# Two chained convolution layers on one core: the square-root table load and one normalisation move to other places

## The chip, the cores and the metric

The kernel runs on one core of a Trainium2 chip. The metric is the time of one execution in microseconds (us); less is better. Engines go by the names that the profile gives them: PE (TensorE, matrix products), DVE (VectorE), ACT (ScalarE), POOL (GpSimd), SP (the engine that issues most transfers).

## The reference

The input x has 16 images of 32 channels, 48 by 48 pixels. Two layers follow one another, each a normalisation over 16 groups of 2 channels (`_gn`), a convolution and an addition to its input:

```python
x = x + _L0_conv_ref(_gn(x), L0_conv_weight, L0_conv_bias)   # 9x9, kernels are Gaussians made from 3 numbers each
x = x + _L1_conv_ref(_gn(x), L1_conv_weight)                 # 5x5, reflected at the edges
...
m = jnp.mean(g, axis=(2, 3, 4), keepdims=True)
s = jnp.var(g, axis=(2, 3, 4), keepdims=True)
return ((g - m) / jnp.sqrt(s + eps)).reshape(v.shape)
```

The Gaussian kernels are computed in the kernel: sine and cosine, an exponential over 9x9 taps, a sum per kernel and a division by it.

## The kernel before, in words

The images are worked in four quads of four (`qd` 0 to 3). Partitions hold 4 row phases of 32 channels. Each layer uses a Winograd form along the rows: layer 1 turns the normalised rows `P` into 8 streams (`s32_1`, shown as `s`), multiplies each with its own weights and combines 8 products into 6 rows. Streams and weights are split into a high and a low half in 16 bits (`hi`, `lo`; `wh`, `wl`, which are both in `whl`), and PE adds the products hi x wh, lo x wh and hi x wl. In the trace a cast `hi<-s` on ACT makes a high half (`high_half`), a subtraction `lo<-s,hi` on DVE the low one (`low_half`). For weights it is `whl<-work` or `whl<-arg` on ACT (`high_kernel`, line 1182) and the same names on DVE at line 568 (`low_kernel`).

Every engine has its instructions in an order written out by hand, and the engines wait for one another with semaphores. Nothing reorders them when the kernel runs.

The change lies in the first quad, where nothing of the weights is ready yet. There the streams are made in the order 1, 2, 0, 7, 3, 4, 5, 6, each as soon as it can be. PE takes for each stream first the five taps that were made ("made": 15 products, three times five), later the four that mirror others ("turned": 12 products). The order on PE starts with stream 1 made, two products that turn its weights around (line 1533), stream 2 made, the same turning for stream 2, stream 1 turned, stream 0 made, and so on. Stream 6 made is the seventh of the made ones, and its high half is the last that ACT makes in this quad (`high_half(1, 0, 7)`).

Streams 1 and 2 of the first quad aren't formed from `P`. PE sums rows of x in the banks (`near_rows`), and ACT (`first_stream1`, line 1118) and DVE (`first_stream2`, line 699) only scale them. All other streams need `P`, which ACT writes in `normalise1` (line 1131), two instructions for each of the four images of the quad. `norm_done[1]` counts the images, and DVE waits for four before `first_half`.

The scale `gsc` and the offset `gof` of the first quad come from the variance. DVE takes the reciprocal square root by a first guess from the bits of the number and further steps (`first_guess`, `first_newton`, `second_root`, `first_scales`), and these small steps stand between the larger sums over the weights (`outer_blocks`, `all_blocks`, `tap_pairs`). For every later quad, `small_stats` on DVE waits for a square root that ACT makes (`standard_deviation`, line 1104), and takes a reciprocal and one Newton step. The table that ACT needs for the square root is loaded once, at line 1278, just ahead of `high_half(1, 0, 7)`. `small_stats(1, 1)` stands on DVE ahead of `low_half(1, 0, 7)`.

POOL normalises the last image of the second quad (line 1393).

Of the kernel before, what the change touches and what calls it, by code (L numbers as in the profile page):

```python
# [26 lines left out]
ALU = mybir.AluOpType  # L27
# [14 lines left out]
IMG = 2  # L42
# [48 lines left out]
NF = len(OUT_FACTORS)  # L91
EPS = 1e-5
ROUND = 12582912.0
ROOT_BITS = float(0x5F3759DF + 6 * 2**23)
ROOT3 = 0.375 ** 0.5
TWO_PI = 6.2831850
SMALL = 9

# [53 lines left out]
def build(nc, x, w0, bias, w1, tables, out):  # L152
    with ExitStack() as ctx:
# [182 lines left out]
        def block1(b):  # L336
            return ker[:, :, b * P:(b + 1) * P]
# [100 lines left out]
        def _(dve):  # L438
# [159 lines left out]
            def step(ins):  # L598

                step_count[0] += 1  # L600
                ins.then_inc(first_step_done, 1)

            def step_landed():
                dve.wait_ge(first_step_done, step_count[0])
# [10 lines left out]
            def first_variance():  # L615
                dve.wait_ge(stat_mm, 1)
                step_landed()
                step(tt(var[1][:, :], STAT[1][:, QI:], msq[1][:, :], ALU.add))
                step_landed()
                step(ts(vare[1][:, :], var[1][:, :], 0.0, EPS, ALU.max, ALU.add))  # L620

            def first_guess():
                step_landed()
                step(ts(rcp[1][:, :].bitcast(I32), vare[1][:, :].bitcast(I32), -0.5, ROOT_BITS, ALU.mult, ALU.add))
                step_landed()
                step(stt(msq[1][:, :], vare[1][:, :], -0.5 / (X_SCALE * X_SCALE), rcp[1][:, :], ALU.mult, ALU.mult))

            def first_newton():
                step_landed()
                step(tt(var[1][:, :], msq[1][:, :], rcp[1][:, :], ALU.mult))  # L630
                step_landed()
                step(stt(rcp[1][:, :], var[1][:, :], 1.5, rcp[1][:, :], ALU.add, ALU.mult))

            def second_root():

                step_landed()
                step(stt(msq[1][:, :], vare[1][:, :], ROOT3 / (X_SCALE * X_SCALE), rcp[1][:, :], ALU.mult, ALU.mult))
                step_landed()
                step(tt(var[1][:, :], msq[1][:, :], rcp[1][:, :], ALU.mult))

            def first_scales():
                step_landed()
                step(stt(msq[1][:, :], var[1][:, :], -1.25 / ROOT3, var[1][:, :], ALU.add, ALU.mult))
                step_landed()
                stt(gsc[1][:, :], msq[1][:, :], 1.875, rcp[1][:, :], ALU.add, ALU.mult).then_inc(small[1], SMALL - 2)
                dve.wait_ge(small[1], SMALL - 2)
                stt(off1[:, :], first_mean, -NEAR_OFFSET, gsc[1][:, :], ALU.mult, ALU.mult).then_inc(small[1], 1)
                stt(gof[1][:, :], first_mean, -1.0, gsc[1][:, :], ALU.mult, ALU.mult).then_inc(small[1], 1)

            def small_stats(c, n):  # L650
# [10 lines left out]
                tt(var[c][:, :], ex2, msq[c][:, :], ALU.add).then_inc(small[c], 1)  # L661
                dve.wait_ge(small[c], at + 3)
                ts(vare[c][:, :], var[c][:, :], 0.0, EPS, ALU.max, ALU.add).then_inc(small[c], 1)
                dve.wait_ge(std_done[c], n + 1 if c == 2 else n)
                nc.vector.reciprocal(rcp[c][:, :], std[c][:, :]).then_inc(small[c], 1)

                dve.wait_ge(small[c], at + 5)
# [24 lines left out]
            def first_stream2():  # L692

                dve.wait_ge(near_mm, 2)
                dve.wait_ge(s_done[1], 1)
                for h in range(2):
                    at = slice(h * TILES1, (h + 1) * TILES1)
                    by_image = gsc[1][:, h * IMG:(h + 1) * IMG].unsqueeze(1).unsqueeze(3).to_broadcast([P, TILES1, IMG, W])
                    ins = tt(by_image1(s32_1[:, 2, :])[:, at, :, :], by_image1(banks[:, NEAR_BANK[2], 0:OUTN])[:, at, :, :], by_image, ALU.mult)
                ins.then_inc(s_done[1], 1)  # L700

            def first_half(key, which, one, other):

# [158 lines left out]
            def first_quad():  # L862
# [7 lines left out]
                outer_blocks(0)  # L870
                first_variance()
                all_blocks(0)
                first_guess()
                outer_blocks(1)
                first_newton()
                all_blocks(1)
                second_root()
                tap_pairs()
                first_scales()
                kernel_sum()  # L880
# [5 lines left out]
                kernel_scale()  # L886
                low_half(1, 0, 0)
                scaled(block1(1), "block1")
                first_stream2()
                low_kernel(1)  # L890
                made_two()
                low_half(1, 0, 1)
                low_kernel(2)
                scaled(block1(0), ("weights", 0))
# [181 lines left out]
        def _(act):  # L1076
# [156 lines left out]
            near_factors((0,))  # L1233
            channel_sums(1, 0, range(2, 4))
            kernel_exponentials()
            near_factors((1, 2))
            opposite_rows()
            first_stream1()
            high_half(1, 0, 0)
            normalise1(0, range(2))  # L1240
            high_kernel(1)
            normalise1(0, range(2, 3))
            high_half(1, 0, 1)
            high_kernel_two()
            turned_kernel(1, 0)
            normalise1(0, range(3, 4))
            turned_kernel(1, 1)
            high_kernel(0)
            turned_kernel(2, 0)
# [24 lines left out]
            turn_kernel(5, wh)  # L1274
            high_kernel(6)
            turn_kernel(5, wl)

            nc.scalar.activation(warm[:, :], bias_c[2][:, :], ACT.Sqrt)
            high_half(1, 0, 7)
            standard_deviation(1, 1)  # L1280
            turn_kernel(6, wh)
# [339 lines left out]
```

## Time and profile before

| | |
|---|---|
| time, median of 3 | 244.48 us (244.37 to 244.97) |
| the profiled execution | 244.16 us |
| its span, from the first to the last instruction | 242.4 us |
| PE busy | 232.7 us, 96% of the span |
| DVE busy | 211.3 us, 87% |
| ACT busy | 154.0 us, 64% |
| mean granted clock of TensorE | 1.000 |

The times are those of whole executions; the trace is of one more execution and shows 1.76 us less between its first and last instruction than its own time. Starts in the trace are counted from the first instruction. Two instructions behind one another on DVE or ACT overlap a little in the trace (the second starts about 0.08 us before the end of the first), so that what one costs its engine is the distance of the starts.

### The profile page before, as it was taken

The page shows a single profiled execution, that of the slowest core. Times are in us where ns is not written, and L with a number is a line of the kernel's source. Part 1 is how long each engine was busy: PE and PEld are TensorE (multiplying, and loading weights), DVE is VectorE, ACT ScalarE, POOL GpSimd, SP SyncE. Part 2 cuts the span into 40 slices and gives each one's busy share as a digit, 9 for nine tenths or more (in the row PEclk, how much of TensorE's full clock was granted, in tenths as well). Part 3 has the DMA queues.
Part 4 walks back from the last instruction along what each step waited for, and adds up shares of the span by engine and source line. Part 5 has one row for each costly group of instructions (what it writes and reads, how often), then busy time and mean ns, then how long its engine had stood idle before and what let it go on. Part 6 is the DMA issues. An engine that isn't in the chain of part 4 may idle for free.

```text
span 242.4 us, 4154 instructions
## 1 busy us (share of the span) xinstructions
PE 232.7 (96%) x1441; PEld 144.9 (60%) x1441; DVE 211.3 (87%) x463; ACT 154.0 (64%) x330; POOL 4.4 (2%) x12
## 2 busy tenths in 40 slices
PE   5997999899999999999999999999999999999995
PEld 5854666555565665555666665556666665655554
DVE  4997999699999999999989998999997459978943
ACT  6858898999399567999537592537359003569210
POOL 1000000050000000000000000000000000000000
DMA  6980031320025000003412000062020001521123
GB/s 212 378 329 1 14 75 45 77 55 0 0 53 159 6 1 0 0 3 101 147 64 97 0 4 0 17 187 108 1 100 0 0 0 48 162 101 55 48 97 97
DMA packets 8709, 17.24 MB, mean 71 GB/s; under 512 B 3312, under 2 KB 5616, under 8 KB 8688
## 3 DMA queue, kind: packets, MB, share of 16 engines
q1 hardware_dynamic: 7712, 16.64, 20.9%
q10 hardware_dynamic: 976, 0.34, 0.6%
q8 instruction: 11, 0.18, 0.3%
q14 instruction: 10, 0.08, 0.1%
HBM read 5.57 MB, written 4.72 MB: 42 GB/s over the span
## 4 chain that ended last, share of the span: by engine, by line
PE 68%; DVE 21%; ACT 6%; issue 4%; DMA 1%; DVEq 0%; ACTq 0%
PE banks L1478 34%; PE banks L1495 33%; DVE X L796 4%; DVE lo L763 2%; DVE whl L568 2%; ACT P L1131 1%; DVE work L563 1%; DMA prm<-in_w 1%; DVE arg L507 1%; DVE s L733 1%; DVE partU L749 1%; ACT whl L1182 1%; DVE s L499 1%; ACT hi L1154 1%; ACT junk L1098 1%
## 5 line engine op out<-in xcount | busy, mean ns | idle before, releaser
L1478 PE MATMUL banks<-hi,whl 128*128 128x360 f16 (+4 forms) x576 | 99.1, 320 | 3.2 <-ACT whl L1182 1.9
L1478 PEld LDWEIGHTS banks<-hi,whl 128*128 128x128 f16 x576 | 55.9, 99 | 38.2 <-ACT whl L1182 2.5
L1478 PE MATMUL banks<-lo,whl 128*128 128x376 f16 (+4 forms) x288 | 51.6, 320 | 0.5 <-DVE lo L763 0.5
L1098 ACT ACTIVATE junk<-X 128x576 bf16<-128x576 f32 x56 | 38.1, 681 | 2.2 <-DVE X L796 0.5
L1478 PEld LDWEIGHTS banks<-lo,whl 128*128 128x128 f16 x288 | 28.0, 98 | 17.8 <-DVE lo L763 1.1
L1495 PE MATMUL banks<-lo,wh 128*128 128x384 f16 (+1 forms) x165 | 31.8, 323 | 0.0
L1495 PE MATMUL banks<-hi,wh 128*128 128x384 f16 (+1 forms) x165 | 31.8, 323 | 0.0
L1495 PE MATMUL banks<-hi,wl 128*128 128x384 f16 (+1 forms) x165 | 31.8, 323 | 0.0
L1154 ACT CAST hi<-work 128x416 f16<-128x416 f32 x32 | 16.6, 538 | 19.9 <-PE banks L1495 14.1
L1154 ACT CAST hi<-s 128x384 f16<-128x384 f32 x32 | 15.3, 508 | 17.8 <-DVE s L730 12.1
L1144 ACT ACTIVATE work<-work,gof,gsc 128x26 f32<-128x26 f32 (+1 forms) x48 | 23.3, 577 | 3.6 <-DVE gof L674 3.6
L1495 PEld LDWEIGHTS banks<-hi,wl 128*128 128x128 f16 x165 | 15.9, 97 | 10.5
L1495 PEld LDWEIGHTS banks<-lo,wh 128*128 128x128 f16 x165 | 15.9, 97 | 10.5
L1495 PEld LDWEIGHTS banks<-hi,wh 128*128 128x128 f16 x165 | 16.0, 98 | 10.4
L763 DVE TENSOR_TENSOR lo<-work,hi 128x416 f16<-128x416 f32 x32 | 17.4, 584 | 1.6 <-ACT hi L1154 1.5
L796 DVE SCALAR_TENSOR_TENSOR X<-pd,X 128x384 f32<-128x384 f32 x36 | 18.1, 558 | 0.0
L796 DVE SCALAR_TENSOR_TENSOR X<-ps,X 128x384 f32<-128x384 f32 x36 | 18.1, 558 | 0.0
L1131 ACT ACTIVATE P<-X,gof,gsc 128x336 f32<-128x336 f32 x30 | 17.7, 658 | 0.5 <-DVE gof L674 0.5
L763 DVE TENSOR_TENSOR lo<-s,hi 128x384 f16<-128x384 f32 x32 | 16.4, 552 | 0.4
L786 DVE SCALAR_TENSOR_TENSOR ps<-banks,mb 128x384 f32<-128x384 f32 x12 | 6.6, 554 | 8.3 <-PE banks L1478 7.6
L1165 ACT ACTIVATE mb<-banks,bias 128x384 f32<-128x384 f32 x12 | 6.9, 572 | 8.2 <-PE banks L1478 8.2
L1098 ACT ACTIVATION_READ_ACCUMULATOR junk<-X 128x1 f32 x56 | 10.5, 187 | 0.0
(141 smaller groups left out, 231.1 us busy)
## 6 DMA issues: line engine op xcount, KB each, us to landing
X<-in_x SPq DMA_DIRECT2D x8, 576.0 KB, 9.5
out<-X SPq DMA_DIRECT2D x7, 576.0 KB, 3.0
work<-X SPq DMA_DIRECT2D x8, 432.0 KB, 3.8
whl<-work SPq DMA_DIRECT2D x24, 64.0 KB, 2.0
work<-X SPq DMA_DIRECT2D x8, 144.0 KB, 3.6
stage<-in_w SPq DMA_DIRECT2D x1, 640.0 KB, 7.2
work<-X SPq DMA_DIRECT2D x32, 12.0 KB, 2.3
out<-X SPq DMA_DIRECT2D x1, 384.0 KB, 2.6
```

Source lines behind the costliest of these rows:

```text
L499: done(tt(ca[:, at, :].rearrange("p k (e o) -> p k e o", o=C), centre.unsqueeze(1).to_broadcast([P, n, NE, C]), ak[:, at, :].unsqueeze(2). ...
L568: tt(made_taps(wl, i), weight1(i), made_taps(wh, i), ALU.subtract).then_inc(wl1_done, 1)
L763: tt(lo[c][:, i, :], src, hi[c][:, i, :], ALU.subtract).then_inc(lo_done[c], 1)
L786: stt(ps[1][:, :], product1(qd, k), f, mb[1][:, :], ALU.mult, ALU.add).then_inc(mid_done[1], 1)
L796: stt(out1(qd, k), tiled1(src[1][:, :]), factors[g][i], out1(qd, k), ALU.mult, ALU.add).then_inc(out_done[1], 1)
L1098: nc.scalar.activation(waste, image(n, m), function, accum_out=sums[c][:, col:col + 1]).then_inc(sums_done[c], 1)
L1131: ins = nc.scalar.activation(dst, src, ACT.Identity, bias=gof[1][:, i:i + 1], scale=gsc[1][:, i:i + 1])
L1144: ins = nc.scalar.activation(dst[:, :, d0:d1_:ds_], src[:, :, s0:s1:ss], ACT.Identity, bias=gof[2][:, i:i + 1], scale=gsc[2][:, i:i + 1])
L1154: nc.scalar.copy(hi[c][:, i, :], src).then_inc(hi_done[c], 1)
L1165: nc.scalar.activation(mb[1][:, :], src, ACT.Identity, bias=bias_c[1 if g == 0 else 2][:, 0:1], scale=FIRST1[g]).then_inc(m_read[1], 1)
L1478: ins = nc.tensor.matmul(dst[:, :, o0:o1], w[1][:, i, t * P:(t + 1) * P], src[:, :, o0 + dx:o1 + dx], start=(first and part == 0 and t == ...
L1495: ins = nc.tensor.matmul(dst, wbuf[2][:, i, j * P:(j + 1) * P], src[:, rows, t:t + W], start=(part == 0 and t == 0), stop=(part == 2 and t ...
```

## The change

It has four parts.

1. The reciprocal square root of the first quad is taken as in later quads. ACT makes the square root, and DVE a reciprocal and one Newton step. The table for the square root is loaded right behind the exponentials of the weights, no longer ahead of `high_half(1, 0, 7)`.
2. ACT normalises one image ahead of `high_kernel(1)`, where it did two, and the others follow later.
3. The fourth image of the first quad (`QI - 1`) is normalised by DVE, with two `tensor_scalar` instructions between `made_two` and `low_half(1, 0, 1)`.
4. On DVE `low_kernel(1)` stands ahead of `first_stream2`.

```diff
-                step(ts(vare[1][:, :], var[1][:, :], 0.0, EPS, ALU.max, ALU.add))
-
-            def first_guess():
-                step_landed()
-                step(ts(rcp[1][:, :].bitcast(I32), vare[1][:, :].bitcast(I32), -0.5, ROOT_BITS, ALU.mult, ALU.add))
+                ts(vare[1][:, :], var[1][:, :], 0.0, EPS, ALU.max, ALU.add).then_inc(small[1], 4)
+
+            def first_root():
+                dve.wait_ge(std_done[1], 1)
+                step(nc.vector.reciprocal(rcp[1][:, :], std[1][:, :]))
                 step_landed()
                 step(stt(msq[1][:, :], vare[1][:, :], -0.5 / (X_SCALE * X_SCALE), rcp[1][:, :], ALU.mult, ALU.mult))
...
-            def second_root():
...
             def first_scales():
-                step_landed()
-                step(stt(msq[1][:, :], var[1][:, :], -1.25 / ROOT3, var[1][:, :], ALU.add, ALU.mult))
-                step_landed()
-                stt(gsc[1][:, :], msq[1][:, :], 1.875, rcp[1][:, :], ALU.add, ALU.mult).then_inc(small[1], SMALL - 2)
+                dve.wait_ge(first_step_done, MARK["first newton"])
+                stt(gsc[1][:, :], var[1][:, :], 1.5, rcp[1][:, :], ALU.add, ALU.mult).then_inc(small[1], SMALL - 6)
...
+            def normalise_last():
+
+                i = QI - 1
+                h, m = i // IMG, i % IMG
+                dve.wait_ge(x_loaded[h], 16)
+                dve.wait_ge(small[1], SMALL)
+                dve.wait_ge(pads_zero, 2)
+                for t in range(TILES1):
+                    dst = P1[:, TILES1 * h + t, :].rearrange("p (r m x) -> p r m x", m=IMG, x=W)[:, 1 - t:ROWS1 - t, m, :]
+                    src = image(h, m)[:, (M1 - 1) * t:(M1 - 1) * t + ROWS1 - 1, :]
+                    ins = ts(dst, src, gsc[1][:, i:i + 1], gof[1][:, i:i + 1], ALU.mult, ALU.add)
+                ins.then_inc(norm_done[1], 1)
...
                 outer_blocks(0)
                 first_variance()
                 all_blocks(0)
-                first_guess()
                 outer_blocks(1)
+                first_root()
+                all_blocks(1)
                 first_newton()
-                all_blocks(1)
-                second_root()
                 tap_pairs()
                 first_scales()
...
                 scaled(block1(1), "block1")
+                low_kernel(1)
                 first_stream2()
-                low_kernel(1)
                 made_two()
+                normalise_last()
                 low_half(1, 0, 1)
...
             kernel_exponentials()
+            nc.scalar.activation(warm[:, :], bias_c[2][:, :], ACT.Sqrt)
+            standard_deviation(1, 0)
             near_factors((1, 2))
...
             high_half(1, 0, 0)
-            normalise1(0, range(2))
+            normalise1(0, range(1))
             high_kernel(1)
-            normalise1(0, range(2, 3))
+            normalise1(0, range(1, 2))
             high_half(1, 0, 1)
             high_kernel_two()
+            normalise1(0, range(2, 3))
             turned_kernel(1, 0)
-            normalise1(0, range(3, 4))
             turned_kernel(1, 1)
...
             turn_kernel(5, wl)
-
-            nc.scalar.activation(warm[:, :], bias_c[2][:, :], ACT.Sqrt)
             high_half(1, 0, 7)
```

The order on ACT, from the exponentials (`arg<-arg`) to the high half of the weights of stream 2 (`whl<-work` with 384 and 256 elements), before the change:

```order
L1178 ACTIVATE arg<-arg 128x768
L1110 ACTIVATE factors<-tab 128x128 x2
L1199 CAST opposite<-tab 128x128
L1118 ACTIVATE s_1<-banks,off,gsc 128x2x48 x4
L1154 CAST hi<-s_1 128x384
L1131 ACTIVATE P<-X,gof,gsc 128x7x48 x4
L1182 CAST whl<-work 128x640
L1131 ACTIVATE P<-X,gof,gsc 128x7x48 x2
L1154 CAST hi<-s_1 128x384
L1188 CAST whl<-work 128x384
L1188 CAST whl<-work 128x256
```

and with the change:

```order
L1179 ACTIVATE arg<-arg 128x768
L1237 ACT_TABLE_LOAD
L1237 ACTIVATE warm<-bias 128x1
L1105 ACTIVATE std<-vare 128x4
L1111 ACTIVATE factors<-tab 128x128 x2
L1200 CAST opposite<-tab 128x128
L1119 ACTIVATE s_1<-banks,off,gsc 128x2x48 x4
L1155 CAST hi<-s_1 128x384
L1132 ACTIVATE P<-X,gof,gsc 128x7x48 x2
L1183 CAST whl<-work 128x640
L1132 ACTIVATE P<-X,gof,gsc 128x7x48 x2
```

A table load and a square root are new behind the exponentials, and the weights of stream 1 (`whl<-work` 128x640) stand behind two normalising instructions, not four.

On DVE, from the scaling of block 1 (`arg<-arg,rs`) to the first part that needs `P` (`partA<-P`), before:

```order
L551 TENSOR_TENSOR arg<-arg,rs 128x5x128
L699 TENSOR_TENSOR s_1<-banks,gsc 128x192 x2
L568 TENSOR_TENSOR whl<-work,whl 128x640
L559 SCALAR_TENSOR_TENSOR work<-arg,work 128x384
L559 SCALAR_TENSOR_TENSOR work<-arg,work 128x256
L763 TENSOR_TENSOR lo<-s_1,hi 128x384
L568 TENSOR_TENSOR whl<-work,whl 128x640
L551 TENSOR_TENSOR arg<-arg,rs 128x5x128
L705 TENSOR_TENSOR partA<-P 128x4x96
```

and with the change:

```order
L549 TENSOR_TENSOR arg<-arg,rs 128x5x128
L566 TENSOR_TENSOR whl<-work,whl 128x640
L687 TENSOR_TENSOR s_1<-banks,gsc 128x192 x2
L557 SCALAR_TENSOR_TENSOR work<-arg,work 128x384
L557 SCALAR_TENSOR_TENSOR work<-arg,work 128x256
L700 TENSOR_SCALAR P<-X,gsc,gof 128x7x48 x2
L764 TENSOR_TENSOR lo<-s_1,hi 128x384
L566 TENSOR_TENSOR whl<-work,whl 128x640
L549 TENSOR_TENSOR arg<-arg,rs 128x5x128
L706 TENSOR_TENSOR partA<-P 128x4x96
```

The two instructions `P<-X,gsc,gof` are new here, and stream 2 (`s_1<-banks,gsc`) stands behind the low half of the weights of stream 1.

On ACT at the end of the quad's weights, where `high_half(1, 0, 7)` is the cast `hi<-s_1` and `standard_deviation(1, 1)` is `std<-vare`, before:

```order
L1182 CAST whl<-work 128x640
L1196 COPY work<-whl 128x512
L1278 ACT_TABLE_LOAD
L1278 ACTIVATE warm<-bias 128x1
L1154 CAST hi<-s_1 128x384
L1104 ACTIVATE std<-vare 128x4
```

and with the change:

```order
L1183 CAST whl<-work 128x640
L1197 COPY work<-whl 128x512
L1155 CAST hi<-s_1 128x384
L1105 ACTIVATE std<-vare 128x4
```

Here the load and the activation behind it are gone.

## Rows read from the trace of the kernel before

**Rows 1.** The page: busy tenths of PE in 40 equal slices of the span

```profile
PE   5997999899999999999999999999999999999995
```

**Rows 2.** Waits of PE, 15 to 60 us: us in total, times, longest us

```profile
PE banks L1478 <- ACT whl L1182: 1.9, 1, 1.9
PE banks L1478 <- ACT hi L1154: 1.2, 2, 0.9
PE banks L1478 <- DVE lo L763: 0.5, 1, 0.5
```

**Rows 3.** Timeline, 44 to 49 us: start us, us, engine, line, operation [idle before]

```profile
45.65 1.28 ACT L1278 ACT_TABLE_LOAD   x1
...
46.14 0.17 DVE L663 TENSOR_SCALAR vare<-var 128x4 f32<-128x4 f32 x1
...
47.05 0.49 ACT L1154 CAST hi<-s 128x384 f16<-128x384 f32 x1
47.45 0.20 ACT L1104 ACTIVATE std<-vare 128x4 f32<-128x4 f32 x1
...
47.69 0.18 DVE L665 RECIPROCAL rcp<-std 128x4 f32<-128x4 f32 x1 [1.38 <-ACT std L1104]
47.90 0.16 DVE L668 SCALAR_TENSOR_TENSOR msq<-vare,rcp 128x4 f32<-128x4 f32 x1
```

**Rows 4.** Timeline of ACT, 9 to 19 us, and PE's start on stream 2

```profile
9.59 1.90 ACT L1178 ACTIVATE arg<-arg 128x1152 f32<-128x1152 f32 x2 [0.54 <-DVE arg L507]
...
14.89 1.40 ACT L1118 ACTIVATE s<-banks,off,gsc 128x96 f32<-128x96 f32 x4 [2.81 <-DVE gof L648]
...
16.74 2.34 ACT L1131 ACTIVATE P<-X,gof,gsc 128x336 f32<-128x336 f32 x4
...
18.98 0.71 ACT L1182 CAST whl<-work 128x640 f16<-128x640 f32 x1
...
22.54 0.95 PE L1478 MATMUL banks<-hi,whl 128*128 128x384 f16 x5
```

**Rows 5.** Timeline of DVE, 12.5 to 15 us

```profile
13.16 0.42 DVE L519 TENSOR_TENSOR work<-work,arg 128x256 f32<-128x256 f32 x1
...
13.77 0.42 DVE L524 TENSOR_TENSOR work<-work 128x256 f32<-128x256 f32 x1
14.10 0.15 DVE L643 SCALAR_TENSOR_TENSOR msq<-var 128x4 f32<-128x4 f32 x1
14.36 0.16 DVE L645 SCALAR_TENSOR_TENSOR gsc<-msq,rcp 128x4 f32<-128x4 f32 x1
...
14.64 0.15 DVE L648 SCALAR_TENSOR_TENSOR gof<-mom,gsc 128x4 f32<-128x4 f32 x1
```

**Rows 6.** Timeline of DVE, 17 to 25 us

```profile
17.45 0.82 DVE L551 TENSOR_TENSOR arg<-arg,rs 128x640 f32<-128x640 f32 x1
18.19 0.61 DVE L699 TENSOR_TENSOR s<-banks,gsc 128x192 f32<-128x192 f32 x2
19.72 0.83 DVE L568 TENSOR_TENSOR whl<-work,whl 128x640 f16<-128x640 f32 x1 [0.92 <-ACT whl L1182]
20.46 0.89 DVE L559 SCALAR_TENSOR_TENSOR work<-arg,work 128x384 f32<-128x384 f32 x2
21.27 0.55 DVE L763 TENSOR_TENSOR lo<-s,hi 128x384 f16<-128x384 f32 x1
...
24.32 0.56 DVE L705 TENSOR_TENSOR partA<-P 128x384 f32<-128x384 f32 x1 [0.79 <-ACT P L1131]
```

**Rows 7.** Groups by line and form, DVE and POOL: busy us, mean ns of one

```profile
L475 DVE TENSOR_TENSOR rnd<-sc 128x64 f32<-128x64 f32 x1 | 0.2, 220 | 0.0
L456 DVE TENSOR_SCALAR rnd<-turn 128x64 f32<-128x64 f32 x1 | 0.2, 195 | 0.0
L582 DVE TENSOR_SCALAR osc<-tab,wpow 128x4 f32<-128x4 f32 x1 | 0.2, 219 | 0.0
L1393 POOL TENSOR_SCALAR P<-X,gsc,gof 128x336 f32<-128x336 f32 x2 | 3.5, 1766 | 47.4 <-DVE gof L674 47.4
```

**Rows 8.** Stretch of an earlier table load: busy us of PE, PEld, DVE, ACT, POOL; PEclk, DMA share, GB/s

```profile
3.80:5.20 1.40, 1.40 (x8) 1.40 (x8) 1.31 (x6) 1.37 (x3) 0.00 (x0) 1.00 1.03 387
```

More of the change, by code:

```diff
@@ L93 @@
 ROUND = 12582912.0
-ROOT_BITS = float(0x5F3759DF + 6 * 2**23)
-ROOT3 = 0.375 ** 0.5
 TWO_PI = 6.2831850
@@ L630, in first_newton @@
                 step(tt(var[1][:, :], msq[1][:, :], rcp[1][:, :], ALU.mult))
-                step_landed()
-                step(stt(rcp[1][:, :], var[1][:, :], 1.5, rcp[1][:, :], ALU.add, ALU.mult))
-            def second_root():
-                step_landed()
-                step(stt(msq[1][:, :], vare[1][:, :], ROOT3 / (X_SCALE * X_SCALE), rcp[1][:, :], ALU.mult, ALU.mult))
-                step_landed()
-                step(tt(var[1][:, :], msq[1][:, :], rcp[1][:, :], ALU.mult))
+                MARK["first newton"] = step_count[0]
             def first_scales():
-                step_landed()
-                step(stt(msq[1][:, :], var[1][:, :], -1.25 / ROOT3, var[1][:, :], ALU.add, ALU.mult))
-                step_landed()
-                stt(gsc[1][:, :], msq[1][:, :], 1.875, rcp[1][:, :], ALU.add, ALU.mult).then_inc(small[1], SMALL - 2)
+                dve.wait_ge(first_step_done, MARK["first newton"])
+                stt(gsc[1][:, :], var[1][:, :], 1.5, rcp[1][:, :], ALU.add, ALU.mult).then_inc(small[1], SMALL - 6)
                 dve.wait_ge(small[1], SMALL - 2)
@@ L663, in small_stats @@
                 ts(vare[c][:, :], var[c][:, :], 0.0, EPS, ALU.max, ALU.add).then_inc(small[c], 1)
-                dve.wait_ge(std_done[c], n + 1 if c == 2 else n)
+                dve.wait_ge(std_done[c], n + 1)
                 nc.vector.reciprocal(rcp[c][:, :], std[c][:, :]).then_inc(small[c], 1)
```

## The prediction, written before the changed kernel ran

> **What bounds the kernel now.** I read the page's slices first. PE is busy in nine tenths or more of every slice from 24 us on, except at the very end [rows 1]. So time can only be won in PE's few waits, or where PE starts. The list of PE's waits names them for 15 to 60 us [rows 2]: 1.9 us for the high half of stream 1's weights, 1.2 us in two waits for a high half of a stream (0.9 the longest), 0.5 us for a low half. The timeline tells where they lie. The first is the start of the convolutions near 19.7 us: ACT casts the weights of stream 1 at 18.98 for 0.71 us [rows 4]. The 0.9 and the 0.5 lie around 47 to 49 us, on one stream: ACT loads a table at 45.65 for 1.28 us, and only then, at 47.05, makes the last high half of the first quad; and the low half of the same stream stands on DVE behind the small statistics, where DVE sat idle 1.38 us for the square root [rows 3]. Between these two places PE doesn't wait, but DVE does hardly either, so it is DVE's lead or lag that arrives at 45 us. DVE's own waits ahead of that are 0.92 us for the same weights and 0.79 us for `P` [rows 6].
>
> I follow three clocks, then: when the weights of stream 1 are cast, by how much DVE is earlier at `partA`, and by how much the low half of the last stream is earlier.
>
> **Part 1, the new root.** The exponentials end at 11.49 [rows 4]. The load starts 0.02 later; the old place took 1.40 us from the load to the next real instruction [rows 3], so the square root starts at 12.91. From there to the reciprocal it took 47.69 - 47.45 = 0.24 and to the next step 0.21 [rows 3]: reciprocal 13.15, next 13.36. The sum `work<-work,arg` follows 0.08 behind, at 13.44, where it stood at 13.16 [rows 5]. It takes 0.42, and the next sum needs its end: 13.87 instead of 13.77. The one Newton product fits beside it. Where there were two steps behind the pair sum (at 0.33 and 0.59 behind it), there is now one, at 0.33: `gsc` at 14.20 instead of 14.36, and `gof` 0.28 later at 14.48 instead of 14.64 [rows 5]. The gain is 0.15 us, for ACT, whose stream 1 starts 0.25 behind `gof` (14.74), and for DVE. The factors and the reversed identity that ACT makes behind the square root come about 1.5 us later than they did, by roughly 13.7, in ACT's idle 2.81 us [rows 4]. The root itself is thus nearly a draw: DVE waits about 0.4 us for it and saves five small steps.
>
> **Part 2, the order on ACT.** Four normalising instructions took 18.98 - 16.74 = 2.24 us, two take 1.12 [rows 4]. The cast starts at 16.74 - 0.15 + 1.12 = 17.71 instead of 18.98, and PE 1.27 us earlier. PE needs the second stream 22.54 - 18.98 = 3.56 behind the cast [rows 4], so at 21.27.
>
> **Parts 3 and 4, DVE to `partA`.** The scaling of block 1 starts at 17.30 and takes 0.74 (the distance of starts, [rows 6]); DVE then waits for the cast, which before it followed 19.72 - 18.98 = 0.74 behind, until 17.71 + 0.74 = 18.45. The low half of the weights takes 0.74 (19.19), stream 2 its 0.61 less the overlap of 0.08, which makes 0.53 (19.72), its weights 0.81 (20.53). Stream 2 now ends at about 19.8, its high half on ACT is there by about 20.3, and PE wants it at 21.27: this new wait of ACT costs nothing, and would cost something only where its cover of 0.9 us were gone.
>
> No row shows a normalisation on DVE. From above, a TENSOR_TENSOR of 64 elements takes 220 ns [rows 7] and one of 384 takes 560 [rows 6], or 506 at 336 elements. A TENSOR_SCALAR of 64 takes 195 [rows 7], less than its neighbour; one of 4 takes 170 [rows 3]. That slope, 0.4 ns an element, gives 310 ns at 336. One whose scalar is a tensor took 219 ns against those 170 [rows 3, 7], so 50 more for the pointers. The bounds are 0.36 and 0.56 us; I take 0.40, since the TENSOR_SCALAR rows lie on the lower slope. Less the overlap the pair costs 0.64 us, at the upper bound 0.95. The Trainium skill, "VectorE: DVE Perf Modes", section "The perf-mode tier table", lets a `tensor_scalar` on fp32 in SBUF run at twice the rate of a `tensor_tensor`, which agrees with the value taken.
>
> DVE goes on at 21.17; the low half takes 0.47, the weights' low half and the next scaling 0.74 each, and `partA` starts at 23.12 instead of 24.32. `P` of the third image is written on ACT by about 22.2, so the wait of 0.79 is gone. DVE is 1.20 us earlier (0.90 by the upper bound), PE 1.27; PE may wait for the difference.
>
> **The end of the quad.** Both engines carry that lead to 45 us. There the load is gone. ACT's high half starts right behind its stream, about 1.4 us earlier beyond the lead; PE doesn't wait for it. The variance starts at 46.14 and ends at 46.31 [rows 3]; the square root could follow 0.04 later and the reciprocal 0.24 after that: 46.59, where it stood at 47.69. So all that hangs on it, `gof`, the last low half and everything of DVE behind, gains 1.10 us beyond the lead. PE comes to that low half earlier by its lead of 1.2 and by the 0.9 us that it no longer waits for the high half, 2.1 in all, and finds it 2.3 earlier: of the wait of 0.5 some 0.4 is left. This wait is what is late next, and so DVE sets the sum, not PE.
>
> **The sum.** 1.20 + 1.10 = 2.30 us, with the upper bound of the normalisation 2.00. From there all engines are earlier by the same amount; the work until about 79 us hangs on DVE and PE as it did, and PE is full afterwards [rows 1]. Against the profiled execution of 244.16 that is 241.86. The median of before lies 0.32 above it, so I forecast 242.2 us.
>
> **The rivals.**
>
> *DVE at one element a cycle* (0.56 us for one normalising instruction): 2.00 us are gained, 242.5. For it: the operand is in rows of 48, and no such row was seen. Against it: the two TENSOR_SCALAR rows. Chance 0.2.
>
> *Only one half arrives.* Either the 1.10 us is eaten where PE, DVE and ACT meet again between 49 and 79 us, or DVE's lead is lost before 45 us because ACT falls behind with its own part; 1.1 or 1.2 us remain, 243.3. For it: DVE runs nearly without a gap there, so a new wait of DVE has no cover. Against it: each wait that I looked at moves with what it waits for. Chance 0.1.
>
> *A dearer load.* At 3.80 to 5.20 us ACT was busy 1.37 of 1.40 us around a load, with the DMA engines full (share 1.03) and the clock at 1.00, the 2.4 GHz level [rows 8]; so a load costs 1.28 us and nothing behind it, also while x is being loaded. If it cost twice that at the new place, the reciprocal, and with it both streams, would come 1.3 us later, and 1.0 us of gain would be left: 243.5. The Trainium skill, "ScalarE: Activation LUTs", section "What ACT_TABLE_LOAD costs", counts a drain of 1.38 us behind each load, 2.66 us in all, and advises to count every switch at that. The rows of this trace don't show the drain: the next real instruction followed 1.40 us behind the start of the load [rows 3]. Chance 0.05.
>
> *Slower.* The one row of this very operation is POOL's, 1766 ns [rows 7]. If DVE needed as much, the pair would cost 2 x 1.69 = 3.38 us, 2.74 more than I count, all of it on the path to `partA`: DVE would be 1.54 us later at `partA` and 0.44 later at the end, 244.9. It decides from 1.55 us for one instruction on. POOL's other durations don't speak for DVE. Chance 0.03.
>
> *No change:* the leads are made, but a transfer or the last low half holds PE where it was. The turned weights go by DMA behind ACT's copies, which move with the rest. Chance 0.04.
>
> **How the numbers follow.** My forecast, with the two-fold rate on DVE, has 0.52: 242.2, and 0.2 us to either side for the estimates in it. More gain than 2.9 us has 0.06: it would need a wait that I count as kept to go, since PE's own lead and its two waits at 47 to 49 us add up to 1.2 + 0.9 + 0.5 = 2.6. The range takes in the one-element case (242.5), the half gains (243.3) and a little below the forecast: 241.6 to 243.4. About 0.3% (0.7 us) is what a measurement of this kernel can tell from no change. Faster by more has 0.92, within it 0.04, slower 0.04.
>
> **What would show it.** The square root near 12.9 and `gof` near 14.5 us; the cast of stream 1's weights near 17.7 and PE's first convolution product near 18.5; `P<-X` on DVE at about 0.4 us each; `partA` near 23.1 with no wait ahead of it; at about 45 to 47 us a single wait of PE, of about 0.4 us, for the low half of the last stream, and DVE's reciprocal near 45.4 with a wait of some 0.3. The prediction is wrong if `partA` is earlier but the reciprocal at the end of the quad isn't, if PE shows a new wait between 20 and 44 us of more than 0.2, or if the lead at 60 us is gone at 100.

## The result, and the profile after

The changed kernel takes 242.06 us (median of 4, 241.99 to 242.10) where the kernel before takes 244.46 us beside it: a ratio of 0.9897, with a 95% interval of 0.9880 to 0.9914. A second measurement on another chip gave 242.59 us (median of 5, 242.02 to 242.85) against 244.43, a ratio of 0.9916 (0.9898 to 0.9935). The forecast was 242.2 us, in a range of 241.6 to 243.4. The profiled execution of the changed kernel took 242.1 us with a span of 240.3.

PE's waits between 15 and 60 us, the view of [rows 2], now read (us in total, times, longest us):

```profile
PE banks L1479 <- ACT whl L1183: 0.6, 1, 0.6
PE banks L1479 <- DVE lo L764: 0.5, 1, 0.5
PE banks L1479 <- ACT hi L1155: 0.3, 1, 0.3
```

The wait for the weights of stream 1 shrank by 1.3 us. Of the two waits for a high half the longer one (0.9) is gone. The wait for the low half is as long as it was.

The timeline of ACT shows the new place of the table load and the order behind it (start us, us, engine, line, operation):

```profile
11.64 1.28 ACT L1237 ACT_TABLE_LOAD   x1
12.93 0.20 ACT L1237 ACTIVATE warm<-bias 128x1 f32<-128x1 f32 x1
13.04 0.19 ACT L1105 ACTIVATE std<-vare 128x4 f32<-128x4 f32 x1
...
14.87 1.40 ACT L1119 ACTIVATE s<-banks,off,gsc 128x96 f32<-128x96 f32 x4 [1.06 <-DVE gof L636]
...
16.72 1.22 ACT L1132 ACTIVATE P<-X,gof,gsc 128x336 f32<-128x336 f32 x2
17.85 0.71 ACT L1183 CAST whl<-work 128x640 f16<-128x640 f32 x1
```

The load takes 1.28 us here too, and 0.12 us behind its end the square root starts. Both lie in what was idle time of ACT: it fell from 2.81 us [rows 4] to 1.06.

The timeline of DVE: its first instruction, the first mean, and from the root to `partA`, which answers to [rows 5] and [rows 6]:

```profile
2.91 0.18 DVE L451 TENSOR_SCALAR turn<-prm 128x32 f32<-128x32 f32 x1 [2.91 <-DMA prm<-in_w]
...
10.54 0.55 DVE L609 TENSOR_REDUCE mom<-banks 128x4 f32<-128x384 f32 x1
...
13.26 0.18 DVE L622 RECIPROCAL rcp<-std 128x4 f32<-128x4 f32 x1 [0.36 <-ACT std L1105]
...
14.62 0.16 DVE L636 SCALAR_TENSOR_TENSOR gof<-mom,gsc 128x4 f32<-128x4 f32 x1
...
18.59 0.82 DVE L566 TENSOR_TENSOR whl<-work,whl 128x640 f16<-128x640 f32 x1 [0.34 <-ACT whl L1183]
19.33 0.62 DVE L687 TENSOR_TENSOR s<-banks,gsc 128x192 f32<-128x192 f32 x2
19.86 0.88 DVE L557 SCALAR_TENSOR_TENSOR work<-arg,work 128x384 f32<-128x384 f32 x2
20.66 0.85 DVE L700 TENSOR_SCALAR P<-X,gsc,gof 128x336 f32<-128x336 f32 x2
21.43 0.55 DVE L764 TENSOR_TENSOR lo<-s,hi 128x384 f16<-128x384 f32 x1
...
23.36 0.55 DVE L706 TENSOR_TENSOR partA<-P 128x384 f32<-128x384 f32 x1
```

DVE waits 0.34 us where it waited 0.92, and not at all ahead of `partA`, where it waited 0.79. The pair `P<-X` costs 21.43 - 20.66 = 0.77 us. DVE's first instruction waits for a transfer (`prm<-in_w`) and starts at 2.91 us; in the trace of before it starts at 2.79, and the first mean at 10.42.

The end of the quad, which answers to [rows 3]:

```profile
44.63 0.51 ACT L1155 CAST hi<-s 128x384 f16<-128x384 f32 x1
...
45.18 0.17 DVE L651 TENSOR_SCALAR vare<-var 128x4 f32<-128x4 f32 x1
45.38 0.20 ACT L1105 ACTIVATE std<-vare 128x4 f32<-128x4 f32 x1 [0.23 <-DVE vare L651]
...
45.62 0.18 DVE L653 RECIPROCAL rcp<-std 128x4 f32<-128x4 f32 x1 [0.27 <-ACT std L1105]
...
47.11 0.96 PE L1479 MATMUL banks<-lo,whl 128*128 128x384 f16 x5 [0.55 <-DVE lo L764]
```

The reciprocal follows the variance by 0.44 us, where it followed by 1.55.

### The profile page after: what moved, and what is told of

Read it like the earlier page. It is cut to its first block, busy times and chain, and to the rows that moved or that the text cites. A ratio compares the mean times of both kernels' runs of the same rounds, so it can differ in the third digit from the quotient of the medians.

```text
span 240.3 us, 4153 instructions
## 1 busy us (share of the span) xinstructions
PE 232.7 (97%) x1441; PEld 144.9 (60%) x1441; DVE 211.6 (88%) x461; ACT 153.2 (64%) x329; POOL 4.4 (2%) x12
## 4 chain that ended last, share of the span: by engine, by line
PE 67%; DVE 23%; ACT 4%; issue 4%; DMA 1%; DVEq 0%; ACTq 0%
PE banks L1479 33%; PE banks L1496 33%; DVE X L797 4%; DVE lo L764 2%; DVE whl L566 2%; DVE work L561 1%; DMA prm<-in_w 1%; DVE s L734 1%; ACT arg L1179 1%; DVE partU L750 1%; DVE s L497 1%; DVE s L737 1%; ACT junk L1099 1%; DVE s L743 1%; DVE arg L549 1%
## 5 line engine op out<-in xcount | busy, mean ns | idle before, releaser
L1132 ACT ACTIVATE P<-X,gof,gsc 128x336 f32<-128x336 f32 x28 | 16.6, 658 | 0.5 <-DVE gof L662 0.5
```

The lines of the kernel that those rows point to most:

```text
L1132: ins = nc.scalar.activation(dst, src, ACT.Identity, bias=gof[1][:, i:i + 1], scale=gsc[1][:, i:i + 1])
```

## How the experiments are compared

Executions of one kernel differ by 0.1 to 1.4 us here, as much as some of the parts. e1 to e4, e5 to e7 and e9 to e12 were measured on three chips, each set beside executions of the kernel before. The changed kernel itself has two medians, 242.06 and 242.59 us, so a median of another set tells little under half a microsecond. So I read four instants in every trace: the start of the first mean on DVE (`mom`, a sum over x that PE makes), of `gof`, of `partA`, and of PE's last group of products. The distances between them don't depend on when the execution started. All are starts in the timelines; "late" is DVE's wait for PE ahead of `mom`.

| kernel | late | mom to gof | gof to partA | partA to PE's last group | lowest time | median |
|---|---|---|---|---|---|---|
| before | 0 | 4.22 | 9.68 | 214.80 | 244.08 | 244.43 to 244.62 |
| changed | 0 | 4.08 | 8.74 | 213.70 | 241.99 | 242.06 |
| e1, part 1 alone | 0 | 4.08 | 9.68 | 213.67 | 242.85 | 243.02 |
| e2, parts 2 to 4 alone | 0.33 | 4.23 | 8.74 | 214.79 | 243.36 | 243.88 |
| e3, stream 2 first | 0 | 4.01 | 8.73 | 213.68 | 241.72 | 242.12 |
| e4, old root, early load | 0.50 | 4.23 | 8.74 | 213.68 | 242.73 | 242.86 |
| e5, before, late sums | 1.00 | 4.24 | 9.68 | 214.79 | 244.22 | 244.68 |
| e6, changed, late sums | 1.34 | 3.63 | 8.96 | 213.68 | 242.06 | 242.54 |
| e7, changed again | 1.10 | 3.63 | 8.97 | 213.66 | 242.02 | 242.59 |
| e9, last image on ACT | 0 | 4.08 | 9.40 | 213.70 | 242.66 | 242.74 |
| e10, DVE's pair twice | 1.09 | 3.63 | 10.01 | 213.69 | 243.01 | 243.13 |
| e11, low half in the wait | 0.48 | 3.64 | 8.95 | 213.44 | 241.78 | 242.02 |
| e12, both orders | 0 | 4.16 | 8.58 | 213.45 | 241.38 | 242.03 |

## The experiments

**e1, part 1 alone.** The order of parts 2 to 4 is undone.

```diff
-                low_kernel(1)
                 first_stream2()
+                low_kernel(1)
                 made_two()
-                normalise_last()
...
-            normalise1(0, range(1))
+            normalise1(0, range(2))
             high_kernel(1)
-            normalise1(0, range(1, 2))
+            normalise1(0, range(2, 3))
             high_half(1, 0, 1)
             high_kernel_two()
-            normalise1(0, range(2, 3))
             turned_kernel(1, 0)
+            normalise1(0, range(3, 4))
             turned_kernel(1, 1)
...
```

> Part 1 alone: the root by ACT and the early table load stay, the order of the normalisations and of stream 2 is that of before. The theory of the prediction (two leads that add up): DVE keeps its waits of 0.92 and 0.79 us ahead of partA and leads there by 0.15 us, and gains 1.10 more at the square root of the second quad: 1.25 us in all, 243.2. The rival (the load was only hidden behind DVE's lateness, so that its removal pays only together with the new order) has 0.2 us or less, 244.3.

It took 243.02 us (ratio 0.9944, 0.9928 to 0.9960). The last distance is 213.67 us, short like that of the whole change, though the middle one is as long as before. So the load's removal from the end of the quad pays without the new order. The rival falls.

**e2, parts 2 to 4 alone.** The kernel before with the new order and DVE's pair; the root and the load stay where they were.

```diff
-                first_stream2()
                 low_kernel(1)
+                first_stream2()
                 made_two()
+                normalise_last()
...
-            normalise1(0, range(2))
+            normalise1(0, range(1))
             high_kernel(1)
-            normalise1(0, range(2, 3))
+            normalise1(0, range(1, 2))
...
```

> Parts 2 to 4 alone: the root by bits and two steps stays on DVE, the table is loaded at its old place ahead of the last high half. The theory: the lead at partA is 1.09 us as measured for the whole change less the 0.15 of the root, 0.94 us, and nothing is won at the end of the quad, where the 1.38 us of idle time of DVE stay: 243.5. The rival (DVE's lead is swallowed by the table load, because ACT is what is late at 45 us): under 0.3 us, 244.2 or more.

It took 243.88 us (ratio 0.9970, 0.9958 to 0.9982). The middle distance is that of the whole change, 8.74, and the last one that of before, 214.79. DVE's lead arrives at the end undiminished and the load's 1.1 us stay: each of the two shows up in its own distance, and the sums of e1 and e2 make the whole. The time is 0.4 us above what I expected; this trace has the first mean 0.33 us late, of which the next runs tell.

**e3, stream 2 ahead of the low half of stream 1's weights** (part 4 alone undone).

```diff
-                low_kernel(1)
                 first_stream2()
+                low_kernel(1)
```

> The whole change, with part 4 alone undone: stream 2 (0.53 us on DVE) stands ahead of the low half of stream 1's weights again. In the changed kernel DVE waits 0.34 us for the cast of these weights, right where stream 2 stood before. The theory: stream 2 fills that wait, the low half of the weights starts some 0.1 us later and all behind it 0.42 us earlier, partA at about 22.95, and the end is 0.4 us earlier, at about 241.65, since PE still waits 0.55 us for the last low half. The rival (part 4 is needed, since PE or ACT would otherwise wait for what moves): as the changed kernel or later, 242.1 or more, with a new wait of PE near 20 us.

It took 242.12 us (ratio 0.9910, 0.9890 to 0.9929; lowest 241.72). The median doesn't bear the theory out. The wait changed its cause: stream 2 now had to wait for PE's sums of rows.

```profile
18.45 0.62 DVE L687 TENSOR_TENSOR s<-banks,gsc 128x192 f32<-128x192 f32 x2 [0.33 <-PE banks L1443]
```

PE's plain sums over x took 4.75 us here and 4.24 in the first trace of the changed kernel, so that the rows ended at 18.42 us and not at 18.01. That is as late as DVE's wait for the cast would have lasted. Part 4 thus gives nothing and costs nothing in this execution.

**e4, the old root with the early load.**

```diff
             kernel_exponentials()
             nc.scalar.activation(warm[:, :], bias_c[2][:, :], ACT.Sqrt)
-            standard_deviation(1, 0)
...
```

> The table is loaded early and the order is the new one, but the first root is made by DVE from bits as before. The theory: the place of the load is what part 1 brings, the root itself only 0.15 us, so gof comes 0.15 us later than in the changed kernel and so does all: 242.2. The rival (DVE's short wait for the square root and the saved steps matter more, or less than nothing): 242.6 or more, or 241.9 or less.

DVE's steps from the bits are back as in the kernel before. It took 242.86 us (ratio 0.9937, 0.9921 to 0.9953), not 0.15 us more than the changed kernel but 0.80 above its first median and 0.27 above its second. The trace has the same middle and last distance. From the first mean to `gof` it is 4.23 us, 0.15 more, as expected; but the first mean itself came 0.50 us late, and the old root passes that on whole. From e2 and e4 came the theory of the next two runs.

**e5 and e6, two more warming products on PE ahead of its sums over x**, in the kernel before and in the changed one. Warming products multiply a table with itself, and nobody reads the result. The two more make PE's sums start at 6.56 us instead of 5.70, and at 6.65 instead of 5.82.

```diff
-WARMING = 6
+WARMING = 8
```

> The kernel before, with two more warming products ahead of PE's plain sums of x (about 1 us of PE time). New theory from the first four runs: the sums over x reach DVE at a time that differs from execution to execution by up to 0.5 us, since x is still arriving. The old root hangs on them by a chain without slack (gof follows the first mean by 4.22 us in each trace), so whatever they are late goes to the end; the new root waits for the table load instead and takes up a lateness of some 0.5 us. Here the sums end about 1 us later, 0.5 us past DVE's arrival: 0.45 us slower than the kernel before. The rival (lateness of the sums is hidden in both kernels alike, or goes through in both alike) has here 0.1 us or 0.5 us, and the same in the changed kernel.

> The changed kernel with the same two more warming products. New theory: the lateness is taken up ahead of the reciprocal, where DVE waited 0.36 us for the square root, and PE's later start (near 19.0 us, 0.4 later) is covered because DVE sets the end of the quad: within 0.15 us of the changed kernel without them in the same call. The rival: 0.45 us or more slower, as in the kernel before.

**e7, the changed kernel again**, beside e5 and e6.

> The changed kernel as it is, on the same chip and beside the same runs of the kernel before as the other three. The prediction's sum has 2.3 us less than before, the first measurement 2.40, the two traces 2.1. New theory: 2.05 us plus what the kernel before loses by late sums, which its own scatter shows (244.19 to 245.16 us in the last call): 2.1 to 2.5 us, with less scatter than the kernel before. Rival (the 0.3 us between trace and median is chance): 2.05 us and the same scatter.

The times were 244.68 us (ratio 1.0010, 0.9995 to 1.0026), 242.54 (0.9924, 0.9903 to 0.9944) and 242.59. The times alone decide nothing. The 0.25 us of e5 lies within the interval. e6 is as fast as e7, as the theory had it, but it may be so because e7's sums were late too in some executions, with no product added: in its traced execution (242.78 us) they were.

```profile
11.27 0.28 PE L1413 MATMUL banks<-sums,tab 128*128 128x4 f32 x2
...
11.47 0.56 DVE L609 TENSOR_REDUCE mom<-banks 128x4 f32<-128x384 f32 x1 [1.10 <-PE banks L1428]
...
12.87 0.17 DVE L618 TENSOR_SCALAR vare<-var 128x4 f32<-128x4 f32 x1
13.76 0.17 DVE L622 RECIPROCAL rcp<-std 128x4 f32<-128x4 f32 x1
...
15.10 0.15 DVE L636 SCALAR_TENSOR_TENSOR gof<-mom,gsc 128x4 f32<-128x4 f32 x1
...
15.57 0.76 ACT L1119 ACTIVATE s<-banks,off,gsc 128x96 f32<-128x96 f32 x2 [1.70 <-PE banks L1443]
```

The plain sums took PE 5.55 us here and 4.21 in the profile of before; DVE stood still for 1.10 us. The reason is in the two traces. From 6 to 8 us PE worked off twice as many of these products in the kernel before (first line) as in e7 (second line); from 9 to 11 us e7 has the full rate too (third line). The columns are busy us of PE with the count of its products, granted clock, DMA share and GB/s:

```profile
6.00:8.00 2.00, 2.00 (x14) 1.00 0.84 304
6.00:8.00 2.00, 2.00 (x7) 1.00 0.85 306
9.00:11.00 2.00, 2.00 (x14) 1.00 1.02 417
```

The transfers moved nearly the same bytes in both. So x isn't what most of the lateness comes from. In all traces the starts of these products are about 320 ns apart at first and 163 ns later. What differs is when the distance halves: near 6.0 us in the kernel before, near 8.8 in e7, and between 6.0 and 9.1 us over all thirteen traces. One product at the slower rate costs 0.16 us. In the kernel before one of the 23 distances is a long one, in e7 eight are, in e10 nine. The late arrival of x adds to it: in e7 the first distance is 479 ns, and the sums start at 5.89 us instead of 5.70. In e1 and e12 PE waited 0.2 and 0.3 us for x in the middle of the sums.

With its sums late DVE no longer waits for the square root, so the way from the mean to `gof` is 3.63 us and not 4.08; but then ACT waits for PE's rows, which are late as well, and 0.22 us go back between `gof` and `partA`. Of a lateness of about 1 us the new root takes up 0.45, of which 0.23 is left at `partA`. The old root keeps its 4.22 to 4.24 us from the mean in all four traces. So the theory is right in kind and was too large. e7's gain of 1.84 us lies outside the 2.1 to 2.5 that it gave, and the smaller scatter isn't shown: 0.83 us over 5 executions against 1.23 over 17.

**e8, the price of the operation that no row of before showed.** Twenty-one instructions behind the last one on DVE, which rewrite the tile `P` when nobody needs it; a part of them:

```diff
...
+                for _ in range(3):
+                    stage_end()
+                    done(ts(to[:, 0:7, 0, :], rows[:, 0:7, 0, :], g, o, ALU.mult, ALU.add))
+                for _ in range(3):
+                    stage_end()
+                    done(ts(to[:, 0:7, 0, :], rows[:, 0:7, 0, :], 0.5, 0.25, ALU.mult, ALU.add))
...
             last_steps()
+            prices()
```

> The changed kernel with 21 instructions behind its last one on DVE, three of each form, each waiting for the one before, which read and write the tile P after its last use: they add some 9 us, and only their durations are of interest. The normalisation of one image took 468 ns on DVE (7 rows of 48 with a pitch of 96, two scalars that are tensors); I had taken 400. Theories: (a) each tensor scalar costs 50 ns or more, then the same form with two constants takes 370 or less; (b) the rows keep it from the doubled rate in part, then 336 elements in one run take 350 to 400 and 14 rows cost more than twice 7 rows less the fixed part; (c) it runs at one element a cycle, then a TENSOR_TENSOR of the same form takes about the same less the scalars, and 14 rows (672 elements) take 350 ns more than 7. At the doubled rate 14 rows take 175 ns more.

The groups by line and form (mean ns of one); 860 and 863 are 14 rows of 48, 866, 848 and 851 are 7 rows of 48, 854 and 857 one run of 336:

```profile
L860 DVE TENSOR_SCALAR P<-P,gsc,gof 128x672 f32<-128x672 f32 x3 | 1.9, 629 | 0.1
L863 DVE TENSOR_SCALAR P<-P 128x672 f32<-128x672 f32 x3 | 1.5, 511 | 0.1
L866 DVE TENSOR_TENSOR P<-P 128x336 f32<-128x336 f32 x3 | 1.5, 508 | 0.1
L848 DVE TENSOR_SCALAR P<-P,gsc,gof 128x336 f32<-128x336 f32 x3 | 1.4, 475 | 0.1
L854 DVE TENSOR_SCALAR P<-P,gsc,gof 128x336 f32<-128x336 f32 x3 | 1.4, 454 | 0.1
L851 DVE TENSOR_SCALAR P<-P 128x336 f32<-128x336 f32 x3 | 1.1, 358 | 0.1
L857 DVE TENSOR_SCALAR P<-P 128x336 f32<-128x336 f32 x3 | 1.0, 335 | 0.1
```

Two scalars that are tensors cost 475 - 358 = 117 ns in rows, 119 in one run and 118 with 14 rows, 59 each. The rows cost 21 to 23 ns against one run. Double the rows take only 153 ns more, 154 with the tensor scalars.
**e9, the last image by ACT again** (part 3 alone undone).

```diff
-                normalise_last()
...
             turned_kernel(1, 0)
+            normalise1(0, range(3, 4))
             turned_kernel(1, 1)
```

> The whole change with part 3 undone: ACT normalises the fourth image, behind the first turned half of stream 1's weights as in the kernel before. The theory (DVE's start on partA decides): DVE saves the pair, 0.77 us, but waits for ACT's fourth image, which ends near 23.95 us in the changed kernel's time; partA 0.6 us later, and all behind it: 0.6 us slower than the changed kernel, that is 1.5 to 1.6 us less than before. The rival (the pair on DVE costs as much as it gives, and the gain comes from ACT's order alone): as the changed kernel, 2.1 us less than before.

It took 242.74 us (ratio 0.9925, 0.9904 to 0.9946), and its lowest time, 242.66, is 0.64 above the lowest of e7. Its gain of 1.86 us lies between the 1.5 to 1.6 of the theory and the 2.1 of the rival, both within the interval, so the trace has to decide. `partA` waits for ACT again:

```profile
24.07 0.56 DVE L706 TENSOR_TENSOR partA<-P 128x384 f32<-128x384 f32 x1 [1.17 <-ACT P L1131]
```

The middle distance is 9.40 instead of 8.74, 0.66 us more with 0.77 us less work on DVE, and the last one is unchanged. The rival falls.

**e10, DVE's pair a second time**, into two tiles that are idle at that time.

```diff
...
+                for t in range(TILES1):
+                    again = (ps, pd)[t][2][:, 0:7 * W].rearrange("p (r x) -> p r x", x=W)
+                    src = image(h, m)[:, (M1 - 1) * t:(M1 - 1) * t + ROWS1 - 1, :]
+                    ts(again, src, gsc[1][:, i:i + 1], gof[1][:, i:i + 1], ALU.mult, ALU.add).then_inc(spare, 1)
```

> The changed kernel with the pair of normalising instructions on DVE done a second time, into a tile that nothing reads at that time: 0.77 us more on DVE ahead of the second low half. The theory (DVE's lead, and not PE's, sets the time): all behind it is 0.7 to 0.8 us later, partA too, and the end by the same amount; PE waits up to 0.8 us in all between 21 and 42 us, where it waited for nothing. The rival (PE or ACT sets the time and DVE has slack): under 0.2 us.

It took 243.13 us (ratio 0.9942, 0.9921 to 0.9962), 0.54 above the median of e7; its lowest time, 243.01, is 1.0 us above the lowest of e7, more than expected. The pair itself was dearer.

```profile
21.51 0.62 DVE L701 TENSOR_SCALAR ps<-X,gsc,gof 128x336 f32<-128x336 f32 x1
22.05 0.61 DVE L701 TENSOR_SCALAR pd<-X,gsc,gof 128x336 f32<-128x336 f32 x1
22.58 0.85 DVE L705 TENSOR_SCALAR P<-X,gsc,gof 128x336 f32<-128x336 f32 x2
```

It occupies 22.58 - 21.51 = 1.07 us instead of 0.77, where its output is one run and its input is in rows. 0.61 us is nearly the 0.51 of a TENSOR_TENSOR plus the 0.12 of two tensor scalars, so the doubled rate is lost. The form of the output is the difference that e8 makes likely as the reason; the tiles differ too. The middle distance grows by 10.01 - 8.97 = 1.04 us against e7, and the last one stays at 213.69. Between 21 and 42 us PE now waits 0.7 us for a low half, where it waited for nothing, as expected:

```profile
PE banks L1484 <- DVE lo L769: 0.7, 1, 0.7
```

What DVE gets ahead of `partA` arrives at the end one for one, here to 0.03 us.

**e11, the last low half in DVE's wait for the square root.**

```diff
                 ts(vare[c][:, :], var[c][:, :], 0.0, EPS, ALU.max, ALU.add).then_inc(small[c], 1)
+                if (c, n) == (1, 1):
+                    low_half(1, 0, 7)
                 dve.wait_ge(std_done[c], n + 1)
...
                 small_stats(1, 1)
-                low_half(1, 0, 7)
                 low_kernel(6)
```

> The changed kernel with the last low half of the first quad moved from behind the small statistics into them, between the variance and the wait for the square root. PE waited 0.55 us for it. The theory (this wait is what is late next): PE's wait goes or shrinks to 0.1 us, the reciprocal comes about 0.1 later, DVE is through with the weights behind it 0.36 us earlier, and the end is 0.35 to 0.45 us earlier than in the changed kernel: about 2.45 less than before. The rival (gof, for which ACT and POOL wait, decides what follows, so that 0.1 us later at gof is 0.1 us later at the end): 0.1 us slower than the changed kernel.

It took 242.02 us (ratio 0.9886, 0.9867 to 0.9906), lowest 241.78. The interval overlaps that of the changed kernel. In the trace PE's wait of 0.55 us is gone, but PE meets two others (idle time and its releaser in the brackets):

```profile
52.68 0.80 PE L1480 MATMUL banks<-hi,whl 128*128 128x376 f16 x4 [0.29 <-DMA whl<-work]
...
55.07 1.57 PE L1480 MATMUL banks<-hi,whl 128*128 128x384 f16 x9 [0.34 <-DVE pd L790]
```

The second quad starts on PE 31.50 us behind `partA`, in the changed kernel 54.85 - 23.36 = 31.49. Up to there nothing is won: the turned weights come by DMA behind a copy of ACT, and ACT is busy without a gap from `gof`, which came 0.10 us later, to the first high half of the second quad. The rival is right for this stretch. Yet the last distance is 0.26 us shorter, 213.44, less than the 0.35 to 0.45 expected. Counted from `partA`, DVE is 0.25 us ahead at 60 us, and PE comes to have that lead between 55 and 77 us. Both theories had a part.

**e12, the same with stream 2 first.**

```diff
-                low_kernel(1)
                 first_stream2()
+                low_kernel(1)
```

> The same with stream 2 ahead of the low half of stream 1's weights as well (part 4 undone). Where the sums of x come in time, stream 2 fills DVE's wait of 0.34 us; where they are late, it waits for PE, as the trace of that change alone showed. The theory: 0.35 to 0.45 us from the low half, and up to 0.4 more in executions whose sums come in time, so the lowest times go down by 0.5 to 0.8 against the changed kernel and the median by about 0.5. The rival (the two gains overlap, since PE's own lead is then the bound): as with the low half alone.

It took 242.03 us (ratio 0.9887, 0.9865 to 0.9910), with the lowest time of all, 241.38. The trace has 8.58 us in the middle and 213.45 at the end, 0.16 and 0.25 less than the changed kernel; stream 2 still waited 0.18 us for PE. The two gains add up there. Against the changed kernel the median is not clearly better; the traces and the lowest time speak for 0.4 to 0.6 us.

## Why the prediction was right

The direction, the size and the way of adding up came out. By its own steps:

- *The new root* was to gain 0.15 us. The distance from the mean to `gof` fell by 0.14 [rows 5]. Over the five traces with the new root and no late sums it is 4.01 to 4.16 us, so the gain is 0.06 to 0.21. The load took 1.28 us at the new place and the square root followed, so the rival of the dearer load is out. In this the rows agree with [rows 8] and not with the drain that the Trainium skill, "ScalarE: Activation LUTs", section "What ACT_TABLE_LOAD costs", counts behind each load.
- *The order on ACT and DVE's pair* were to bring 1.20 us with the root, 1.05 without. The distance from `gof` to `partA` fell by 0.94. The term that was mis-sized is the pair: 0.64 us taken, 0.77 measured. The rate was right, the doubled one. Both parts of one instruction's price were low (e8). The scalars were taken from a row with one such scalar, 50 ns, and this operation has two, 117 ns. The rest was taken as 310 ns, and it measures 358. 1.05 less the 0.13 us of the pair is 0.92, so 0.02 us stay unexplained.
- *The end of the quad* was to gain 1.10 us. The last distance fell by 214.80 - 213.70 = 1.10, and e1 and e2 show that this is the load's place and nothing else.
- *DVE sets the sum, not PE*: shown from both sides, by e9 (0.66 us later at `partA`, the same distance behind it) and e10 (1.04 us). The wait of PE for the last low half stayed, at 0.55 us. I had expected 0.4, and even that was a slip: PE 2.1 us earlier and the low half 2.3 leave 0.3 of 0.5. Measured, the low half came 2.07 us earlier (49.18 to 47.11) and PE was free for it 2.08 earlier.
- *No new wait of PE between 20 and 44 us, and the lead kept*: PE was busy in 24.00 of 24.00 us from 20 to 44. DVE is 2.07 us ahead of the kernel before at 53 us and 2.06 at 100 and at the end.

The sum by the distances is 0.14 + 0.94 + 1.10 = 2.18 us instead of 2.30. The two traced executions differ by 244.16 - 242.10 = 2.06 us, because 0.12 went the other way ahead of the first mean: DVE's first input landed at 2.91 us and not at 2.79. That is also why the instants that I forecast came 0.1 to 0.2 us late (`gof` at 14.62, `partA` at 23.36). The first measurement gave 2.40 and the second 1.84. Both hold 2.18 within their intervals; the lowest times differ by 244.08 - 241.99 = 2.09. That the forecast met the first median to 0.14 us is in part luck.

What I had not seen is that all three distances start at the first mean, and that the mean needs PE's plain sums. In the two traces compared above they were there in time, and DVE's start was set by its own chain. My sum took that as given, since [rows 5] had no wait there. In seven of the thirteen traces (all but that of e8) DVE waited for the mean 0.3 to 1.3 us, in five of them without added products. In those five the run of long distances at the start of PE's plain products (290 ns or more) has five to nine of the 23; in the six traces without a wait it has one to four.

Left open: why PE comes to 163 ns near 6 us in one execution and near 9 in another. The granted clock is 1.00 in both stretches, and no run changes this by itself. Nor is it settled whether e4's six executions, all at 242.73 us or more, are explained by late sums alone. Its one trace explains 0.15 us by the root and 0.50 by the sums. Holding the sums early, by another order of the loads or a shorter sum, wasn't tried.

## What to carry to other kernels

Where the first stage of a kernel is a race of several chains and the rest is one long chain, cut the trace at the instants where the chains meet and compare distances: that told 0.14, 0.94 and 1.10 us apart where medians scatter by half a microsecond. A table load belongs where its engine is idle; 1.28 us in such a place cost nothing (e4 against e2 from the mean to `gof`: 4.23 us in both), and 1.10 us came back from the place where two engines waited for it. Price an operation with the number of its tensor scalars, and give input and output the same shape.

## What the runs showed of the hardware

- A scalar that is a tensor costs DVE 59 ns in a TENSOR_SCALAR (358 against 475 ns for two of them).
- The doubled rate of a TENSOR_SCALAR on 32 bits holds with seven rows on both sides (358 ns without tensor scalars) and was lost when the seven rows went into one run (e10: 612 to 617 ns with two of them, against 464 to 473).
- The time of PE's 24 plain products over x (192 columns, fp32) went from 4.21 to 5.65 us between executions of these kernels. Their starts are about 320 ns apart at first and 163 ns later, and the change came between 6.0 and 9.1 us. The profile's granted clock is 1.00 at both rates and doesn't show it.
